# An attention and MLP kernel: three changes of order in the attention, and one product moved as a pair

## What is computed

```python
x = x + attn(layernorm(x), Wq, Wk, Wv, Wo, Wg1, Wg2, norm_weight)
x = x + ffn(layernorm(x), ...)     # weights packed in 4 bits, width 4096

# attn, 16 heads of 32, chunks of 128 rows:
q, k, v = x @ Wq, x @ Wk, x @ Wv;  q, k = rotate(silu(q)), rotate(silu(k))
scores = (q @ k.T) * D                          # D: decay mask within a chunk
o = scores @ v + (q * decay_q) @ S              # S: the 32x32 state of a head
S = lam_C * S + (k * decay_k).T @ v
gate = x @ Wg1 @ Wg2                            # Wg1: 512 x 32, Wg2: 32 x 512
o = groupnorm_rms(o * sigmoid(gate)) * norm_weight
return o @ Wo
```

## Time and profile before

| | |
|---|---|
| median of 3 runs | 1288.63 us (1288.62 to 1290.58) |
| the profiled execution | 1288.75 us, span 1286.7 us |
| TensorE busy | 1270.3 us, 99% of the span |
| VectorE, ScalarE, GpSimd busy | 917.0, 475.2, 435.2 us |

### The profile page before, as it was taken

One profiled execution on the slowest core, in us unless ns is written; L12 is line 12 of the kernel. 1 busy time (PEld: TensorE's weight loads), 2 busy tenths in 40 slices (PEclk: granted clock), 3 DMA queues, 4 the chain that ended last, 5 costly groups with the idle time before them and its releaser, 6 DMA issues.

```text
span 1286.7 us, 20699 instructions
## 1 busy us (share of the span) xinstructions
PE 1270.3 (99%) x7376; PEld 1043.5 (81%) x7376; DVE 917.0 (71%) x1594; ACT 475.2 (37%) x799; POOL 435.2 (34%) x360
## 2 busy tenths in 40 slices
PE   9999999998999999999999999999999999999998
PEld 6888888887788888888888888888888888888887
DVE  7878788788867667676767676767767666767665
ACT  5433434434433333333333433333333333333421
POOL 2434455564442322223132324133232324232400
PEclk9999999999999999999999999999999999999999
DMA  9000000000001000010000000001001000000003
GB/s 326 12 2 1 19 17 2 2 1 2 25 25 33 17 33 27 22 33 28 29 24 24 24 24 24 33 16 33 24 24 33 24 33 24 24 24 24 24 13 119
DMA packets 21778, 40.23 MB, mean 31 GB/s; under 512 B 2660, under 2 KB 2916, under 8 KB 21604
## 3 DMA queue, kind: packets, MB, share of 16 engines
q1 hardware_dynamic: 21060, 39.47, 9.4%
q10 hardware_dynamic: 672, 0.13, 0.1%
HBM read 35.40 MB, written 4.19 MB: 31 GB/s over the span
## 4 chain that ended last, share of the span: by engine, by line
PE 93%; DVE 2%; POOL 1%; ACT 1%; issue 1%; POOLq 0%; DVEq 0%; ACTq 0%
PE bank L1351 16%; PE bank L1354 15%; PE bank L1353 15%; PE bank L1197 13%; PE bank L1199 13%; PE bank L1198 13%; PE bank L1211 2%; PE bank L1291 1%; PE bank L1310 1%; PE bank L1300 1%; PE bank L1343 1%; PE bank L1331 1%; PE bank L1258 0%; ACT xg L394 0%; PE bank L1257 0%
## 5 line engine op out<-in xcount | busy, mean ns | idle before, releaser
L883 DVE TENSOR_TENSOR acc<-acc,bank 128x512 f32<-128x512 f32 x248 | 169.3, 683 | 129.4 <-PE bank L1199 129.3
L1197 PE MATMUL bank<-wdh,hh 128*128 128x512 f32 x512 | 199.3, 389 | 0.0
L1199 PE MATMUL bank<-wdh,hl 128*128 128x512 f32 x512 | 199.2, 389 | 0.0
L1198 PE MATMUL bank<-wdl,hh 128*128 128x512 f32 x512 | 199.2, 389 | 0.0
L1351 PE MATMUL bank<-xoh,wgh 128*128 128x512 f32 x448 | 175.9, 393 | 0.6 <-DVE cxa L891 0.6
L1351 PE MATMUL bank<-xoh,wuh 128*128 128x512 f32 x448 | 175.1, 391 | 0.7 <-ACT cxa L482 0.7
L1354 PE MATMUL bank<-xoh,wgl 128*128 128x512 f32 x448 | 174.5, 390 | 0.0
L1354 PE MATMUL bank<-xoh,wul 128*128 128x512 f32 x448 | 174.3, 389 | 0.0
L1353 PE MATMUL bank<-xol,wuh 128*128 128x512 f32 x448 | 174.3, 389 | 0.0
L1353 PE MATMUL bank<-xol,wgh 128*128 128x512 f32 x448 | 174.3, 389 | 0.0
L899 DVE TENSOR_TENSOR hl<-hx,hh 128x512 fp32r<-128x512 f32 x128 | 113.5, 887 | 51.4 <-ACT hh L489 51.0
(11 more groups left out here) (163 smaller groups left out, 2285.7 us busy)
## 6 DMA issues: line engine op xcount, KB each, us to landing
stg<-packed_dram SPq DMA_DIRECT2D x48, 256.0 KB, 2.5
stg<-scales_dram SPq DMA_DIRECT2D x48, 256.0 KB
out_dram<-acc SPq DMA_DIRECT2D x16, 256.0 KB, 2.0
acc<-x_dram SPq DMA_DIRECT2D x3, 1024.0 KB, 15.0
w_in<-wq_dram SPq DMA_DIRECT2D x2, 512.0 KB, 5.2
w_in<-wk_dram SPq DMA_DIRECT2D x2, 512.0 KB, 6.9
w_in<-wv_dram SPq DMA_DIRECT2D x2, 512.0 KB, 8.6
w_in<-wo_dram SPq DMA_DIRECT2D x2, 512.0 KB, 11.2
```

The lines of the kernel that those rows point to most:

```text
L883: V.tensor_tensor(row, row, BY[j % 2][:], ALU.add).then_inc(y_add, 1)
L1197: pe.matmul(dst, w_h, x_h, start=start, stop=False)
L1198: pe.matmul(dst, w_h, x_l, start=False, stop=False)
L1199: return pe.matmul(dst, w_l, x_h, start=False, stop=stop)
```

## The change

Four edits are made, all in the attention.

The gate's first product takes the high and low part of the input together. Both now lie in one tile, `xt` (and `ot`), and `gate1` makes 4 matmuls with 256 moving columns: 128 of the high part and 128 of the low. The two partial sums stand side by side in BS[3]; ScalarE copies the first into `gs` (`gate_copy`, behind the silu), VectorE adds the second (`sum_gate`, ahead of the rotation), and both `gate_low` read the sum from `gs`. The scores, which overwrite BS[3], wait for `gate_sum` instead of `g_lo`.

`o_transpose(t-1)` stands ahead of `v_project(t+1)`. In `passage` it did already.

`o_back(t)` stands behind the first block of the q projection where c < 3.

ScalarE's `ot_hi_` moves ahead of its `gate_low` and `v_copy`, VectorE's `gate_low` behind the rotation.

```diff
@@ ScalarE
             def gate_low(t):
+                act.wait_ge(gate_sum, t + 1)
+                act.wait_ge(gate_ps, t)
+                A(g4h[96:128, :], gs[96:128, 1, :], ACT.Copy)
+                A(g4[0:96, :], gs[0:96, 1, :], ACT.Copy).then_inc(g_hi, 1)
+
+            def gate_copy(t):
+
                 act.wait_ge(g1_ps, t + 1)
-                act.wait_ge(gate_ps, t)
-                A(g4h[96:128, :], BS[3][96:128, 0:P], ACT.Copy)
-                A(g4[0:96, :], BS[3][0:96, 0:P], ACT.Copy).then_inc(g_hi, 1)
+                act.wait_ge(gate_sum, t)
+                A(gs[:, 0, :], BS[3][:, 0:P], ACT.Copy).then_inc(g1_sb, 1)
...
                 silu_qk(t + 1)
-                gate_low(t + 1)
+                gate_copy(t + 1)
                 if at_start(b, c):
                     xt_hi_(2)
+                if not at_start(b, c):
+                    ot_hi_(t - 1)
+                gate_low(t + 1)
                 v_copy(t + 1, (c + 1) % 2)
                 if not at_start(b, c):
-                    ot_hi_(t - 1)
                     xt_hi_(t + 2)
@@ VectorE
+            def sum_gate(t):
+
+                dve.wait_ge(g1_sb, t + 1)
+                dve.wait_ge(g_hi, t)
+                V.tensor_tensor(gs[:, 1, :], gs[:, 0, :], BS[3][:, P:2 * P], ALU.add
+                                ).then_inc(gate_sum, 1)
...
                 decayed_q(t)
-                gate_low(t + 1)
+                sum_gate(t + 1)
                 if at_start(b, c):
                     xt_lo_(2)
                 rope_of(b, c, t + 1, (c + 1) % CHUNKS)
+                gate_low(t + 1)
                 if not at_start(b, c):
                     ot_lo_(t - 1)
@@ TensorE
                 pe.wait_ge(gate_tanh, t)
-                xh, xl = x_of(t)
+                x = ot if isinstance(t, int) and t == 1 else xt
                 for k in range(KT):
-                    g1 = g1s[:, k, :, :].rearrange("p r d -> p (r d)")
-                    pe.matmul(BS[3][:, 0:P], g1, xh[:, k, :], start=(k == 0), stop=False)
-                    ins = pe.matmul(BS[3][:, 0:P], g1, xl[:, k, :], start=False,
-                                    stop=(k == KT - 1))
+                    ins = pe.matmul(BS[3][:, 0:2 * P].rearrange("p (a t) -> p a t", a=2),
+                                    g1s[:, k, :, :].rearrange("p r d -> p (r d)"), x[:, :, k, :],
+                                    start=(k == 0), stop=(k == KT - 1))
                 ins.then_inc(g1_ps, 1)
...
                 else:
+                    o_transpose(t - 1)
                     pe.wait_ge(st_done, kvs(b, c))
                 v_project(t + 1)
-                if not at_start(b, c):
-                    o_transpose(t - 1)
...
-                pe.wait_ge(g_lo, t + 2)
+                pe.wait_ge(gate_sum, t + 2)
...
-                if c < CHUNKS - 1:
-                    o_back(t)
                 q_ready(t + 2)
                 for k in range(KT):
-                    if c == CHUNKS - 1 and k == 2:
+                    if k == (1 if c < CHUNKS - 1 else 2):
                         o_back(t)
                     q_part(k)
```

More of the change, by code:

```diff
@@ L119, in build @@
             xn = sb("xn", [P, 512], F32, att)
-            xth = sb("xth", [P, KT, P], F32R, att)
+            gs = sb("gs", [P, 4, P], F32, att)
             sq = sb("sq", [P, 512], F32, att)
-            oth = sb("oth", [P, KT, P], F32R, att)
+            kd = sb("kd", [P, 512], F32, att)
             wo_h = sb("wo_h", [P, KT, 512], F32R, att)
@@ L128, in build @@
             qa = sb("qa", [P, 2, 512], F32, att)
-            xtl = sb("xtl", [P, KT, P], F32R, att)
-            kd = sb("kd", [P, 512], F32, att)
+            xt = sb("xt", [P, 2, KT, P], F32R, att)
             g1s = sb("g1s", [P, KT, 4, HD], F32R, att)
@@ L144, in build @@
             pr = sb("pr", [P, QB, 512], F32, att)
-            otl = sb("otl", [P, KT, P], F32R, att)
+            ot = sb("ot", [P, 2, KT, P], F32R, att)
             nw = sb("nw", [P, KT], F32, att)
@@ L150, in build @@
             rr = sb("rr", [P, HEADS], F32, att)
+            xth, xtl = xt[:, 0, :, :], xt[:, 1, :, :]
+            oth, otl = ot[:, 0, :, :], ot[:, 1, :, :]
             g1_in = pr[:, 1, 0:KT * HD].rearrange("p (k d) -> p k d", k=KT)
@@ L212, in build @@
         qk_ps, g1_ps, v_ps, gate_ps = sem("qk_ps"), sem("g1_ps"), sem("v_ps"), sem("gate_ps")
+        g1_sb, gate_sum = sem("g1_sb"), sem("gate_sum")
         g_hi, g_lo = sem("g_hi"), sem("g_lo")
@@ L355, in xt_hi_ @@
                 if t == 1:
-                    A(oth[:], BO[:].rearrange("p (k t) -> p k t", k=KT), ACT.Copy
+                    A(oth, BO[:].rearrange("p (k t) -> p k t", k=KT), ACT.Copy
                       ).then_inc(xt_hi, 1)
@@ L360, in xt_hi_ @@
                     act.wait_ge(v_ps, 1)
-                    A(xth[:], BO[:].rearrange("p (k t) -> p k t", k=KT), ACT.Copy
+                    A(xth, BO[:].rearrange("p (k t) -> p k t", k=KT), ACT.Copy
                       ).then_inc(xt_hi, 1)
@@ L364, in xt_hi_ @@
                 act.wait_ge(v_ps, t)
[L365 removed]
+                A(xth, BV[:].rearrange("p (k t) -> p k t", k=KT), ACT.Copy).then_inc(xt_hi, 1)
             def gate_low(t):
+                act.wait_ge(gate_sum, t + 1)
[3 more added lines that the diff above has]
+            def gate_copy(t):
                 act.wait_ge(g1_ps, t + 1)
[L369 to L371 removed]
+                act.wait_ge(gate_sum, t)
+                A(gs[:, 0, :], BS[3][:, 0:P], ACT.Copy).then_inc(g1_sb, 1)
             def silu_qk(t):
@@ L403, in ot_hi_ @@
                 act.wait_ge(wo_ps, t)
-                A(oth[:], BO[:].rearrange("p (k t) -> p k t", k=KT), ACT.Copy).then_inc(ot_hi, 1)
+                A(oth, BO[:].rearrange("p (k t) -> p k t", k=KT), ACT.Copy).then_inc(ot_hi, 1)
             def wide_hi(k, n, dst, piece):
@@ L429, in _ @@
             silu_qk(0)
+            gate_copy(0)
             xt_hi_(1)
@@ L500, in passage @@
                 silu_qk(t)
+                gate_copy(t)
                 gate_low(t)
@@ L672, in xt_lo_ @@
                 if t == 1:
-                    V.tensor_tensor(otl[:], BO[:].rearrange("p (k t) -> p k t", k=KT),
-                                    oth[:].bitcast(F32), ALU.subtract).then_inc(xt_lo, 1)
+                    V.tensor_tensor(otl, BO[:].rearrange("p (k t) -> p k t", k=KT),
+                                    oth.bitcast(F32), ALU.subtract).then_inc(xt_lo, 1)
                     return
                 if t == 2:
-                    V.tensor_tensor(xtl[:], BO[:].rearrange("p (k t) -> p k t", k=KT),
-                                    xth[:].bitcast(F32), ALU.subtract).then_inc(xt_lo, 1)
+                    V.tensor_tensor(xtl, BO[:].rearrange("p (k t) -> p k t", k=KT),
+                                    xth.bitcast(F32), ALU.subtract).then_inc(xt_lo, 1)
                     return
-                V.tensor_tensor(xtl[:], BV[:].rearrange("p (k t) -> p k t", k=KT),
-                                xth[:].bitcast(F32), ALU.subtract).then_inc(xt_lo, 1)
+                V.tensor_tensor(xtl, BV[:].rearrange("p (k t) -> p k t", k=KT),
+                                xth.bitcast(F32), ALU.subtract).then_inc(xt_lo, 1)
+            def sum_gate(t):
[3 more added lines that the diff above has]
+                                ).then_inc(gate_sum, 1)
             def gate_low(t):
                 dve.wait_ge(g_hi, t + 1)
-                V.tensor_tensor(g4[96:128, :], BS[3][96:128, 0:P], g4h[96:128, :].bitcast(F32),
+                V.tensor_tensor(g4[96:128, :], gs[96:128, 1, :], g4h[96:128, :].bitcast(F32),
                                 ALU.subtract).then_inc(g_lo, 1)
@@ L709, in ot_lo_ @@
                 dve.wait_ge(ot_hi, t + 1)
-                V.tensor_tensor(otl[:], BO[:].rearrange("p (k t) -> p k t", k=KT),
-                                oth[:].bitcast(F32), ALU.subtract).then_inc(ot_lo, 1)
+                V.tensor_tensor(otl, BO[:].rearrange("p (k t) -> p k t", k=KT),
+                                oth.bitcast(F32), ALU.subtract).then_inc(ot_lo, 1)
             def add_x1(t):
@@ L787, in _ @@
             dve.wait_ge(s_rot, 16)
+            sum_gate(0)
             rope_of(None, 0, 0, 0)
@@ L925, in passage @@
                 decayed_q(s)
+                sum_gate(t)
                 gate_low(t)
@@ L1469, in passage @@
                 pe.wait_ge(xg_done, s)
-                pe.wait_ge(g_lo, t + 1)
+                pe.wait_ge(gate_sum, t + 1)
                 for g in range(KT):
```

1 line of the change is left out of this document (removed).

## The result

| | |
|---|---|
| changed kernel | 1297.29 us, median of 4 runs (1296.72 to 1298.04) |
| kernel before, beside it | 1288.62 us, median of 4 runs (1288.38 to 1290.58) |
| ratio | 1.0061 (95% interval 1.0046 to 1.0076) |
| the profiled execution | 1296.72 us, span 1294.7 us |
| predicted | 1290.8 us, range 1285.2 to 1294.8 |

So 0.6% slower where no change was the likeliest: 8.7 us by the medians, 8.0 us by the two profiled spans, where +2.1 stood in the sum. The kernel before was run beside each set of experiments; two executions, one of `trans_only` (3288.6 us) and one of the kernel before in the third set (4117.49), stand far apart from all others and are left out of the ratios.

A forecast was written before the change was run, and what follows sets the result against it. TensorE, busy for 1270.3 of 1286.7 us, was taken to bound the kernel. Gains of 6.0 + 4.1 = 10.1 against losses of 12.2 gave net +2.1 on 1288.75, so 1290.8 us, range 1285.2 to 1294.8.

The forecast's parts named there:

- Part 1: Gate's first product as 4 matmuls of 256 columns: block 0.45 us, saving 0.40 in 15 tiles, 6.0 us.
- Rival C: Gate's product: 256 columns cost what 512 do, no saving, stalls shrink by 2.4; +5.7 us, 1294.5; chance 0.04.
- Part 2: Turn back (o_back) behind the first q block: 3.74 us against 4.15, saving 0.41 ten times, 4.1 us.
- Rival D: Turn back: the q block doesn't hide the copy xg, the 4.1 us are gone; +4.6, 1293.4; chance 0.07.
- Part 3: Transpose ahead of v waits for sq: stalls 1.3, 1.05, 0.75, 0.8 more in passage, and two of 4.0 us.
- Chain and gate move together: First tile, gate at 43.00: VectorE's chain shifts as the gate does, leaving a stall for sq of 1.3 us.
- rival A: Gates at 170.90 and 207.58: no collision, stalls of 1.8 to 2.0 each; 1286.9 down to 1285.7; chance 0.34.
- unchanged otherwise: Gates at 170.90 and 207.58, L703's end as now: stalls for sq of 2.0 to 2.8 and 2.0 us.
- the collision: Gates at 170.90 and 207.58: GpSimd's L1051 blocks VectorE's last small step and L703; stalls 4.0 each, 8.0 us.
- Part 4: ScalarE's added copy and VectorE's sum, 0.3 us each per tile: cost nothing, at most 9.6 us if uncovered.
- Rival B: Stalls as long as 4 us lower TensorE's clock in two tiles, 2.8 us each, +5.6; 1296.4; chance 0.17.

The follow-up runs named there:

- trans_only: Kernel before with only the transpose of the former output moved ahead of v, and ScalarE's copy for it; 1293.45 us, ratio 1.0033.
- back_only: Kernel before with only the turn back moved behind the first block of q in ten tiles; 1286.62 us, ratio 0.9986.
- low_late: Changed kernel with VectorE's gate_low moved behind the masks; 1299.87 us, ratio 1.0075.
- pair_back: Changed kernel with the transpose of the former output put back behind v, and ScalarE's copy for it; 1288.90 us, ratio 1.0002.
- best1: pair_back with VectorE's gate_low moved behind the masks; 1287.53 us, ratio 0.9983.
- kept_busy: Changed kernel with unused matmuls ahead of the early transpose, 16 in tile 1 and 11 in tile 10; 1293.19 us, ratio 1.0033.
- best2: best1 with GpSimd's rotation also waiting until sq is done (on_done); 1282.52 us, ratio 0.9946.
- pool_after_sq: Changed kernel with GpSimd's first rotation waiting until sq is done (on_done); 1291.29 us, ratio 1.0011.
- low_pool: Changed kernel with VectorE's gate_low behind the masks and GpSimd's rotation waiting for on_done; 1291.56 us, ratio 1.0017.
- best3: best2 with passage in the same order: transpose behind v, gate_low behind the masks; 1281.29 us, ratio 0.9938.

## Why the prediction was wrong, point by point

- **Part 1, the pair's width: right.** 0.47 to 0.48 for four matmuls of 256 columns, 0.45 forecast. Fifteen times 0.37 is 5.5 us instead of 6.0. Rival C is out.
- **Part 2, the turn back: right.** 3.73 against 3.74, no wait for `xg`, and `back_only` shows the 4.1 us. Rival D is out.
- **Part 3, stalls for `sq`: the method right, the places wrong.** Tiles 5 and 13 came at 1.02 and 0.78 (1.05 and 0.75), `passage` at 1.34 (1.43), the other tiles at 0.19 together (0.3). Tile 1 has 4.0 instead of 1.3. "Chain and gate move together" failed there: the gate stayed at 42.99, and VectorE's last `wo_l` step was issued at 38.78, behind GpSimd's L1086 at 38.64, and took 1.55 instead of 0.74, so that `gated` starts at 40.25 instead of 39.59; the last small step then met L1073 by 0.08 us. In tile 8 `sq` escaped L1073 by 0.08 us, as TensorE was late by the terms below, and the stall was 1.56: there rival A's case came true. In tile 10 L1073 came 0.11 ahead of `sq`, which took 1.71, and the stall was 2.76. Together, with `passage`, 11.0 of stalls beyond those of before were measured, 12.2 forecast. The total was near by luck: three places each hang on a tenth of a microsecond. A side figure was misread too: by the part's own rows the stall of tile 8, "unchanged otherwise", is 174.16 - 170.95 = 3.2 and not 2.0 to 2.8; the sum doesn't use it. `low_late`, in which 4.25 and 4.0 come in tiles 8 and 10, shows that the collision itself was read rightly.
- **Part 4, "I cost them at nothing": the step that failed first.** The added copy and sum were priced, with the place where they hide. The operation that was only moved was not: VectorE's gate low part, placed in the 1.25 us of idle time ahead of L710, the time in which I had already hidden the sum. Moreover its first operand is no longer PSUM but the SBUF tile `gs`, so that it is blocked by GpSimd: 1.26 us in tile 3 instead of 0.30. The Trainium skill, SBUF — State Buffer, Who interferes with whom, says that a VectorE instruction with at most one SBUF input doesn't contend with GpSimd and one with two does; I applied it to `sum_gate` and not to the instruction that reads the sum. The trace agrees in both (0.29 and 1.26). Cost: 9.65 against the 5.34 of `trans_only`, in which no low part is late, 4.3 us in eight tiles, and some 7 in the thirteen tiles of `pair_back` (13.9 against 6.6). The sum had this term at 0.
- **Rival B, the clock, had 0.17 and happened; its condition was wrong.** It was tied to "as long as 4 us", and it takes less: the clock fell behind idle times of 3.8 and 2.6 in this kernel, of 2.2 in `trans_only`, of 1.55 and 1.36 in `best1`. So it had to be a term of the sum, and it stood at 0 there. The price per v projection was right by the half: 1.5 each (4.44 - 2.93) and not 2.8, since the clock comes back before v ends. Together 3.1 us, and 0.9 behind `passage`. The stated range ended at 1294.8 although B's own sum gave 1296.4. That this is near the measured 1297.29 is luck, as B had too much for the clock and nothing for the late low part.
- **Not foreseen, a gain:** the transpose ahead of v and v take 3.31 in `trans_only` instead of 3.37, and the transposes of x behind the scores 0.41 instead of 0.48, together 0.7 + 1.3 us over the tiles. The pair has a gain of its own there: 3.28 in `pair_back`, with the transpose behind v; in the changed kernel the two don't add up.

With the two wrong steps put right the sum is: +2.1, +4.3 for the late low part, +3.1 and +0.9 for the clock, 1.2 less of stalls, 2.0 less by the gain just named, 0.5 more for the pair: 7.7 against the 8.0 measured. All of these terms were read from the traces afterwards; it is an account and not a forecast.

The 0.9 behind `passage` is the clock: `kept_busy` has the same program there and a clock of 1.00, and from the transposes of q and k in `passage` (307.42 in the changed kernel, 304.66 there) to the end of the span it takes 986.4 us instead of 987.3; the kernel before takes 986.5 (from 300.24).

What stays open: what makes the clock fall behind one idle time and not behind another. In the profiled runs it fell behind 1.36, 1.5 (`best2`, `pool_after_sq`), 1.55, 2.2, 2.6 and 3.8 us, and in the changed kernel's `passage` behind two waits of 1.1 and 1.0; it didn't fall behind 2.0 and 2.1 in `low_pool`, 1.8 in `pool_after_sq` and 1.5 in `best3`. So no length of the stall alone decides, and runs of one program differ.

## What to carry to other kernels

When a change moves an instruction, price it at the new place as if it were new: who runs beside it there, whether its operands now come from SBUF, and which idle time it uses up, counting each idle time only once. An order that makes a saturated TensorE wait for a chain of small VectorE steps is a bet on tenths of a microsecond, and it can be lost twice, since behind a stall TensorE can run at half the clock for a while, for another 1.5 us here. Stalls of 1.4 us were enough for that in some runs. Such a fall makes the runs of one kernel differ by 1 to 4 us, so that a difference of this size needs many runs, with their granted clocks beside them. If another engine's instruction can be held back until the chain is through at no cost of its own (GpSimd's wait here: 6.0 us), do that before anything is moved.
